# Phase 2 of a two-layer kernel: value products in three rounded passes, scalings and mixes moved to ScalarE, a new order on every engine

## The chip, the cores and the metric

The kernel runs on one core of one Trainium2 chip. The metric is device time in microseconds (us). The program is written as one instruction stream per engine: TensorE (PE in the profile; its weight loads are PEld), VectorE (DVE), ScalarE (ACT), GpSimd (POOL) and SyncE (SP), which only issues transfers here. Each stream runs strictly in its written order, and streams wait for each other through semaphores. TensorE writes only into PSUM, of which there are eight banks of 128 x 512 in float32.

## The reference

The input is 16 x 512 tokens of width 128. Everything that the change touches lies behind the slot softmax of the first layer, whose exponentials are ready when phase 2 begins. `_silu(y)` is y times sigmoid(y).

```python
xn = _layernorm(x)
Q = xn @ Wq + bq                      # K = V = Q, per sequence of 512 tokens
s = softmax(Q @ Q.T / sqrt(128)) @ Q
y = einsum('tznp,npH->tzH', C, Y_tilde)     # 2048 slots mixed into each token
x = x + s * _silu(y)
xn = _layernorm(x)
# layer 1, per sequence: gated linear recurrence
i_t, r_t = sigmoid(xn @ W_ig + b_ig), sigmoid(xn @ W_rg + b_rg)
a_t = exp(8 * r_t * log(sigmoid(lam) + 1e-8))
h_t = a_t * h_{t-1} + sqrt(1 - a_t**2 + 1e-6) * i_t * (xn @ W_in)
s = rmsnorm(h) @ W_out
xr = mu_r * xn + (1 - mu_r) * x_prev       # x_prev: xn one token earlier
xk = mu_k * xn + (1 - mu_k) * x_prev
g = sigmoid(xr @ W_r) * (relu(xk @ W_k)**2 @ W_v)
x = x + s * _silu(g)
```

## The kernel before

The work has three phases. The first two build the experts' outputs (`YHI`, `YLO`) and store the slot exponentials to device memory. Phase 2, which the change rewrites, starts at about 630 us of the profiled run and lasts to the end. It goes over 16 blocks of 512 tokens, software-pipelined: while TensorE mixes the slots of block n, the recurrence of blocks n-1 and n-2 is worked on.

For a block there are 16 chunks of 128 slots. Chunk c is loaded by SP, weighted by POOL (`exps_weighed`, two chunks at a time, line 142), turned by four transposes on TensorE into one of two PSUM banks `ct` (`exps_turned`, line 1094), rounded to float32r by ACT (`chunk_high`, line 1346, into a ring `chi` of RC = 4 buffers), its remainder taken by DVE (`chunk_low`, line 1505, into `clo`), and multiplied by three rounded matmuls (`combine`, lines 1104, 1105 and 1107: high x high, low x high, high x low). `exps_turned(c)` waits until `chunk_low(c - 2)` has released the bank.

Attention: `project` makes Q in bank `at[0]`, ACT copies it with the bias (`query`, line 1294), DVE rounds it (`project_split`), POOL takes the remainder (`query_low`), `values` (line 1126) turns it on TensorE into `at[1]` and waits for `query`; `scores(r)` are three rounded matmuls for each of four row groups, `row_max` (DVE), `probabilities` (ACT, Exp, line 1309, with a read of the row sum), `weights` (DVE reciprocal), `scaled` (DVE, line 1531), `turn(k)` transposes (line 1154), `turn_high(k)` (ACT copy, line 1317), `weigh(k)`: one float32 matmul (line 1164), which counts as two records.

Recurrence: `mean` (float32 matmul, line 1171), `centre` (DVE, line 1550), `squares`, `variance` (float32, line 1179), `deviation_log` (Ln, line 1356), `deviation_inverse` (Exp, line 1361), `normalise`, `normalised_split`, `normalised_low`, `difference` (POOL, line 1716), `mix_r`, `mix_k` (DVE, lines 1571 and 1578), three gate products of three rounded matmuls each (`decay_gate`, `input_gate`, `input_product`), float32 products `ffn_k`, `ffn_r`, `ffn_v`, `state_mean`, `state_out`, the scan (DVE, line 1614), and the pointwise steps on ACT (`decay_tanh`, `decay` (line 1373), `input_tanh` (line 1387), `input_log` (Ln, line 1417), `input_root` (Exp), `state_log` (Ln), `state_inverse`, `ffn_tanh`, ...).

The order of the streams is written out by hand or by a planner as five plain lists of calls in one loop per engine (lines 1070, 1230, 1451, 1645 and 1736); nothing reorders them.

## Time and profile before

| what | us |
|---|---|
| median of 3 runs | 1239.2 (1236.46 to 1244.97) |
| profiled execution, its own time | 1248.32 |
| its span, first to last instruction | 1246.5 |
| PE busy | 1162.2 (93%) |
| DVE busy | 1091.1 (88%) |
| ACT busy | 888.1 (71%) |
| POOL busy | 985.5 (79%) |

The busy time of an engine is a union of its instructions' durations. Instructions of one engine overlap by a little (the next starts before the one before has ended), so what an instruction costs its engine is read from start to start in the timeline, not from its duration. The granted TensorE clock averaged 0.972 of full speed over the span.

### The profile page before, as it was taken

Reading aid. Unit: us, or ns where it says so; the run is one execution under the profiler, and the core shown is the slowest. Engines: PE = TensorE matmul, PEld = TensorE weight load, DVE = VectorE, ACT = ScalarE, POOL = GpSimd, SP = SyncE. Lnnn points to the kernel's source line nnn. Section 1 sums busy time; section 2 is a strip of 40 time slices with the busy share of each in tenths; the row PEclk is TensorE's granted clock in tenths of the full one; section 3 lists DMA queues with packets and bytes.
Section 4 is the critical chain, followed back from the end, with each engine's and each line's share of the span. In section 5 each row is a group of like instructions: output and inputs, shape, how many; then the busy total and the mean of one; then the engine's idle time right before and its main releaser. Section 6 shows DMA issues by size and latency. Waiting matters only on the chain.

```text
span 1246.5 us, 17321 instructions
## 1 busy us (share of the span) xinstructions
PE 1162.2 (93%) x4994; PEld 776.7 (62%) x4994; DVE 1091.1 (88%) x1578; ACT 888.1 (71%) x2001; POOL 985.5 (79%) x790
## 2 busy tenths in 40 slices
PE   2799999999999999999689999999999999999984
PEld 2465556666666666665267777776677766777751
DVE  4799999999999999998457889999989889999873
ACT  4577777776766666666457887876787877788764
POOL 3499888999999999999467788877798777778720
PEclk9799999999999999999789999999999999999997
DMA  5444344443433434343734343434343434434310
GB/s 141 157 150 150 142 151 150 152 157 136 148 138 133 153 133 150 135 150 134 237 102 146 125 140 115 147 116 135 116 147 109 146 111 149 137 120 145 114 39 17
DMA packets 125486, 167.35 MB, mean 134 GB/s; under 512 B 7504, under 2 KB 101712, under 8 KB 125392
## 3 DMA queue, kind: packets, MB, share of 16 engines
q1 hardware_dynamic: 124720, 165.18, 39.7%
q10 hardware_dynamic: 672, 1.06, 0.3%
q8 instruction: 41, 0.67, 0.2%
q14 instruction: 53, 0.43, 0.1%
HBM read 90.71 MB, written 75.50 MB: 133 GB/s over the span
## 4 chain that ended last, share of the span: by engine, by line
PE 38%; DVE 7%; issue 4%; ACT 1%; POOL 0%; DVEq 0%; ACTq 0%; POOLq 0%
PE ct L1094 7%; PE at L1164 4%; PE yac L1107 4%; PE yac L1105 4%; PE yac L1104 4%; PE at L1154 2%; DVE b_e L1531 2%; DVE clo L1505 2%; PE lp L1210 1%; PE lp L1204 1%; PE lp L1216 1%; PE at L1143 1%; PE at L1142 1%; PE at L1140 1%; PE lp L1222 1%
## 5 line engine op out<-in xcount | busy, mean ns | idle before, releaser
L142 POOL TENSOR_TENSOR exp_slots_loaded<-exp_slots_loaded,slot_max 128x1024 f32<-128x1024 f32 x128 | 333.8, 2627 | 52.9 <-DMA exp_slots_loaded<-exp_slots 52.3
L813 POOL TENSOR_TENSOR dd<-ed,rz 128x512 f32<-128x512 f32 x256 | 264.7, 1050 | 39.5 <-ACT rz L659 37.7
L547 PE MATMUL acc<-dd,xns 128*128 128x512 f32 x512 | 262.5, 595 | 2.2 <-POOL dd L813 2.2
L1505 DVE TENSOR_TENSOR clo<-ct,chi 128x512 fp32r<-128x512 f32 x256 | 172.6, 679 | 58.6 <-ACT chi L1346 57.6
L824 POOL TENSOR_TENSOR ch<-exp_slots_loaded 128x512 f32<-128x512 f32 x128 | 164.1, 1282 | 26.7 <-ACT exp_slots_loaded L637 26.7
L751 DVE TENSOR_REDUCE mr<-lg 128x16 fp32r<-128x512 f32 x256 | 167.5, 686 | 19.9 <-PE lg L504 19.5
L628 ACT ACTIVATE ed<-lg 128x512 f32<-128x512 f32 x256 | 142.1, 594 | 55.7 <-PE lg L528 55.7
L637 ACT ACTIVATE exp_slots_loaded<-lg 128x512 f32<-128x512 f32 x256 | 147.9, 591 | 26.4 <-PE lg L535 23.3
L1346 ACT ACTIVATE chi<-ct 128x512 fp32r<-128x512 f32 x256 | 150.3, 594 | 20.3 <-PE ct L1094 19.2
L535 PE MATMUL lg<-shift_experts_to_slots,mt 128*128 128x512 f32 x256 | 162.7, 656 | 0.5 <-ACT ed L628 0.5
L1094 PEld LDWEIGHTS ct<-identity,exp_slots_loaded 128*128 128x128 f32 x1024 | 126.0, 142 | 57.7 <-issue 21.6
L1094 PE MATMUL ct<-identity,exp_slots_loaded 128*128 128x128 f32 x1024 | 153.0, 275 | 6.4 <-DVE clo L1505 3.5
L767 DVE TENSOR_REDUCE zd<-ed 128x32 f32<-128x1024 f32 x128 | 154.8, 1209 | 1.3 <-ACT ed L628 1.3
L760 DVE TENSOR_REDUCE mr<-lg 128x32 fp32r<-128x1024 f32 x128 | 155.8, 1217 | 0.0
L502 PE MATMUL lg<-phi_then_expert_out,xn_transposed 128*128 128x512 f32 x256 | 131.4, 513 | 12.3 <-PEq L395 12.0
L1104 PE MATMUL yac<-chi,phi_then_expert_out 128*128 128x512 f32 x256 | 132.6, 518 | 0.0
L547 PEld LDWEIGHTS acc<-dd,xns 128*128 128x128 f32 x512 | 94.1, 189 | 23.5 <-issue 3.9
L1107 PE MATMUL yac<-clo,phi_then_expert_out 128*128 128x512 f32 x256 | 102.5, 400 | 4.6 <-DVE clo L1505 4.6
L504 PE MATMUL lg<-phi_then_expert_out,xn_transposed 128*128 128x512 f32 x256 | 102.1, 399 | 0.0
L503 PE MATMUL lg<-phi_then_expert_out,xn_transposed 128*128 128x512 f32 x256 | 102.0, 398 | 0.0
L1105 PE MATMUL yac<-chi,phi_then_expert_out 128*128 128x512 f32 x256 | 101.9, 398 | 0.0
L535 PEld LDWEIGHTS lg<-shift_experts_to_slots,mt 128*128 128x128 f32 x256 | 48.3, 189 | 74.5 <-ACT ed L628 44.0
(200 smaller groups left out, 2435.5 us busy)
## 6 DMA issues: line engine op xcount, KB each, us to landing
exp_slots<-exp_slots_loaded SPq DMA_DIRECT2D x128, 512.0 KB, 2.8
exp_slots_loaded<-exp_slots SPq DMA_DIRECT2D x128, 512.0 KB, 3.9
xns<-xn_rows SPq DMA_DIRECT2D x128, 64.0 KB, 2.6
expert_w<-in_expert_w SPq DMA_DIRECT2D x8, 512.0 KB, 5.9
b_xraw<-in_xT SPq DMA_DIRECT2D x16, 256.0 KB, 3.7
out_t<-b_ti SPq DMA_DIRECT2D x16, 256.0 KB, 2.1
xn_rows<-slot_sum SPq DMA_DIRECT2D x8, 256.0 KB, 4.7
slot_sum<-in_x SPq DMA_DIRECT2D x2, 512.0 KB, 6.7
```

What stands on the lines that cost most here:

```text
L142: e.tensor_tensor(rows, rows, joined(SM, b)[:, h].unsqueeze(2).broadcast_to([P, TPB, GC * EPC, NP]), ALU.mult).then_inc(s_we)
L535: e.matmul(lg[v % 2][:, bank(k)], mt[v % 2][:, :], S2M[:, bank(k)], start=False, stop=True, skip_group_check=True).then_inc(s_s2)
L547: e.matmul(acc[k][:, :], xns[v % RX][:, :], dd[v % RX][:, bank(k)], start=tile == 0, stop=tile == NT - 1, skip_group_check=True).then_inc( ...
L751: e.tensor_reduce(mr[v % 2][:, k * HN // 2:(k + 1) * HN // 2], lg[v % 2][:, bank(k)].rearrange("q (n p) -> q n p", p=NP), AX_X, ALU.max).t ...
L760: e.tensor_reduce(mr[v % 2][:, HN:G], lg[v % 2][:, :].rearrange("q (n p) -> q p n", p=NP), AX_X, ALU.max).then_inc(s_mx)
L767: e.tensor_reduce(zd[v % 2][:, :], ed[v % RD][:, :].rearrange("q (n p) -> q n p", p=NP), AX_X, ALU.add).then_inc(s_zd)
L813: e.tensor_tensor(dd[v % RX][:, bank(k)].rearrange("q (n p) -> q n p", p=NP), ed[v % RD][:, bank(k)].rearrange("q (n p) -> q n p", p=NP), ...
L824: e.tensor_tensor(ch[v % 2][:, :], ec[v % RE][:, 0:BANK], ec[v % RE][:, BANK:HS], ALU.add).then_inc(s_ch)
L1094: done = e.transpose(ct[c % 2][:, rows(k)], ECL[:, g // GC % RL, k, c % GC * P:(c % GC + 1) * P], IDENT[:, :])
L1104: e.matmul(yac[:, :], YHI[:, c, :], chi[c % RC][:, :], start=c == 0, stop=False)
L1107: e.matmul(yac[:, :], YHI[:, c, :], clo[c % RC][:, :], start=False, stop=c == CH - 1).then_inc(c_y)
L1505: e.tensor_tensor(clo[c % RC][:, :], ct[c % 2][:, :], hi_f32(chi[c % RC][:, :]), ALU.subtract).then_inc(c_l)
```

## The change

It rewrites part of phase 2.

- `weigh(k)` becomes three rounded matmuls: the values and the turned probabilities are each kept as a rounded part and a remainder. New DVE steps take the remainders: `value_low` once and `turn_low` four times per block. `turn` and `values` now wait for the remainder (`kl`) where they waited for the copy (`kh`).
- `scaled` (four per block) moves from DVE to ACT.
- `mean` multiplies by identity minus mean, so its product is the centred input; `centre` is gone, and `squares` and `normalise` read PSUM.
- `difference` (POOL) is gone. ACT multiplies xn by mu (`scaled_r`, `scaled_k`), and DVE's `mix_r`, `mix_k` add (1 - mu) x_prev. Two small DVE instructions prepare 1 - mu before phase 2.
- `y_copy` is gone; `y_tanh` and `silu_y` read the accumulator `yac`, and the next block's `combine(0)` waits for `silu_y`.
- The rings `chi` and `clo` have 3 buffers in place of 4.
- All five orders are new; ACT's has two loads of the Ln set and two of the Tanh set per block in place of one each.

```diff
-            RC = 4
+            RC = 3
@@ combine
-                        e.wait_ge(y_c, i)
+                        e.wait_ge(S["u_y"], i)
@@ weigh
-                    e.matmul(at[0][:, :], B["vf"][:, rows(k)], pt[k % 2][:, :], start=k == 0, stop=k == TPB - 1).then_inc(A["w"])
+                    e.matmul(at[0][:, :], R["vh"][:, rows(k)], pth[k % 2][:, :], start=k == 0, stop=False)
+                    e.matmul(at[0][:, :], R["vl"][:, rows(k)], pth[k % 2][:, :], start=False, stop=False)
+                    e.wait_ge(A["kl"], i * TPB + k + 1)
+                    e.matmul(at[0][:, :], R["vh"][:, rows(k)], ptl[k % 2][:, :], start=False, stop=k == TPB - 1).then_inc(A["w"])
@@ mean
-                        e.matmul(lp[0][:, :], MEAN[:, :], B[f"x1{i % 2}"][:, :], start=True, stop=True).then_inc(S["mn"])
+                        e.matmul(lp[0][:, :], CENTRE, B[f"x1{i % 2}"][:, :], start=True, stop=True).then_inc(S["mn"])
@@ ScalarE: new
+                def scaled(i, r):
+                        e.wait_ge(A["z"], i * TPB + r + 1)
+                        e.activation(B[f"e{r}"][:, :], B[f"e{r}"][:, :], ACT.Identity, bias=one(EPS, 3),
+                                     scale=one(nmx, 4 * r + 3)).then_inc(A["p"])
+                def scaled_r(i):
+                        e.activation(B["xr"][:, :], x_in, ACT.Identity, bias=one(EPS, 3), scale=one(VEC, V_MUR)).then_inc(S["mr"])
...
@@ VectorE: new
+                def value_low(i):
+                        e.wait_ge(S["v_h"], i + 1)
+                        e.tensor_tensor(R["vl"][:, :], at[1][:, :], hi_f32(R["vh"][:, :]), ALU.subtract).then_inc(S["v_l"])
+                def turn_low(i, k):
+                        e.wait_ge(A["kh"], i * TPB + k + 1)
+                        e.tensor_tensor(ptl[k % 2][:, :], at[1][:, :], hi_f32(pth[k % 2][:, :]), ALU.subtract).then_inc(A["kl"])
...
```

The new order of TensorE, one round of its loop (n is the block whose slots are mixed; ET is `exps_turned`, C is `combine`):

```
C12(n-1) C13(n-1) turn2(n-1) ET15(n-1) decay_gate(n-2) C14(n-1) weigh1(n-1) turn3(n-1) C15(n-1)
weigh2(n-1) weigh3(n-1) ET0 input_gate(n-2) ET1 input_product(n-2) project C0 ET2 ffn_k(n-2)
values C1 ET3 C2 scores0 ET4 ET5 ffn_r(n-2) scores1 C3 scores2 ffn_v(n-2) ET6 C4 ET7 scores3
state_mean(n-2) ET8 C5 mean(n-1) C6 ET9 state_out(n-2) C7 variance(n-1) ET10 C8 turn0 ET11 C9
ET12 C10 turn1 ET13 weigh0 ET14 C11
```

The new order of ScalarE from the start of block n (CH is `chunk_high`):

```
CH0 CH1 input_tanh(n-2) log_table input_log(n-2) tanh_table query input_root(n-2) CH2 value_high CH3
CH4 ffn_k_relu(n-2) probabilities0 ffn_r_tanh(n-2) ffn_k_squares(n-2) CH5 next_factors
probabilities1 state_squares(n-2) CH6 scaled0 CH7 ffn_tanh(n-2) log_table probabilities2
state_log(n-2) scaled1 CH8 squares(n-1) probabilities3 state_inverse(n-2) CH9 scaled2 scaled3
deviation_log(n-1) tanh_table CH10 turn_high0 CH11 deviation_inverse(n-1) CH12 CH13 turn_high1 CH14
scaled_r(n-1) turn_high2 CH15 scaled_k(n-1) decay_tanh(n-1) decay(n-1) turn_high3 y_tanh
decay_squares(n-1) attended
```

## Rows read from the trace of the kernel before

**Rows 1.** Stretch of 15 blocks: us; PE, PEld, DVE, ACT, POOL busy; clock; DMA.

```profile
663.50:1206.30 542.80, 533.64 (x2649) 386.69 (x2648) 487.25 (x753) 425.32 (x770) 421.57 (x232) 1.00 0.40 128
```

**Rows 2.** Line 1331, one per block: durations ns min/median/max, first and last start us.

```profile
L1331 ACT ACTIVATE yt<-yac x16: 597/599/603, 663.5 to 1206.3; 128x512 f32<-128x512 f32 x16
```

**Rows 3.** Timeline of PE inside one block: start us, us, instruction, count.

```profile
825.93 0.60 PE L1094 MATMUL ct<-identity,exp_slots_loaded 128*128 128x128 f32 x4
826.37 1.02 PE L1164 MATMUL at<-pt,b_vf 128*128 128x512 f32 x2
827.23 0.60 PE L1094 MATMUL ct<-identity,exp_slots_loaded 128*128 128x128 f32 x4
...
828.76 0.39 PE L1111 MATMUL lp<-r_xl,weights_high 128*128 128x512 f32 x1
828.98 0.40 PE L1112 MATMUL lp<-r_xh,weights_low 128*128 128x512 f32 x1
829.22 0.40 PE L1104 MATMUL yac<-chi,phi_then_expert_out 128*128 128x512 f32 x1
```

**Rows 4.** Timeline of ACT around one table load.

```profile
841.51 0.62 ACT L1338 ACTIVATE b_ty<-yt 128x512 f32<-128x512 f32 x1
842.15 1.28 ACT L1445 ACT_TABLE_LOAD   x1
843.45 0.72 ACT L1417 ACTIVATE b_a<-b_a,epsilons 128x512 f32<-128x512 f32 x1
```

**Rows 5.** Lines of ACT over the same 15 blocks: count, busy us, mean ns, idle before.

```profile
L1445 ACT ACT_TABLE_LOAD x15 | 19.2, 1283 | 0.3
L1449 ACT ACT_TABLE_LOAD x15 | 19.2, 1283 | 0.3
L1373 ACT ACTIVATE b_aa<-b_aa,derived_vectors 128x512 f32<-128x512 f32 x15 | 12.2, 811 | 0.0
L1387 ACT ACTIVATE b_ti<-lp,derived_vectors 128x512 f32<-128x512 f32 x15 | 10.3, 690 | 14.3 <-PE lp L1112 14.3
```

**Rows 6.** Timelines of PE, ACT and DVE: what starts what.

```profile
866.14 0.60 PE L1094 MATMUL ct<-identity,exp_slots_loaded 128*128 128x128 f32 x4
...
866.77 0.60 ACT L1346 ACTIVATE chi<-ct 128x512 fp32r<-128x512 f32 x1 [0.65 <-PE ct L1094]
...
873.48 0.58 ACT L1346 ACTIVATE chi<-ct 128x512 fp32r<-128x512 f32 x1
...
874.09 0.69 DVE L1505 TENSOR_TENSOR clo<-ct,chi 128x512 fp32r<-128x512 f32 x1 [1.26 <-ACT chi L1346]
...
850.62 0.67 DVE L1505 TENSOR_TENSOR clo<-ct,chi 128x512 fp32r<-128x512 f32 x1
...
851.34 0.66 PE L1094 MATMUL ct<-identity,exp_slots_loaded 128*128 128x128 f32 x4 [1.46 <-DVE clo L1505]
```

**Rows 7.** Timeline of ACT, five instructions in a row without idle time.

```profile
853.49 0.69 ACT L1309 ACTIVATE b_e<-at,nmx 128x512 f32<-128x512 f32 x1
854.07 0.19 ACT L1309 ACTIVATION_READ_ACCUMULATOR b_e<-at,nmx 128x1 f32 x1
854.16 0.62 ACT L1351 ACTIVATE b_ty<-b_kr 128x512 f32<-128x512 f32 x1
854.69 0.68 ACT L1432 ACTIVATE b_aa<-lp,epsilons 128x512 f32<-128x512 f32 x1
855.26 1.08 ACT L1346 ACTIVATE chi<-ct 128x512 fp32r<-128x512 f32 x2
```

**Rows 8.** Three DVE lines that read SBUF: ns min/median/max.

```profile
L1531 DVE TENSOR_SCALAR b_e<-b_e,nmx x64: 469/485/2697, 641.8 to 1186.9; 128x512 f32<-128x512 f32 x64
L1578 DVE SCALAR_TENSOR_TENSOR b_xk<-weights,vectors,xn x16: 740/2882/2891, 684.7 to 1225.6; 128x512 f32<-128x512 f32 x16
L1614 DVE TENSOR_TENSOR_SCAN b_hh<-b_aa,vectors,b_ti x16: 1270/1272/3459, 702.9 to 1236.3; 128x512 f32<-128x512 f32 x16
```

**Rows 9.** Busy time by engine at the end of the run, columns as in the first group.

```profile
1200.00:1246.00 46.00, 23.85 (x57) 11.58 (x55) 18.45 (x27) 25.30 (x36) 3.51 (x3) 0.76 0.03 12
```

More of the change, by code:

```diff
@@ L1136, in scores @@
                     elif r == 1:
[L1137 removed]
+                        e.wait_ge(S["v_l"], i + 1)
                     else:
@@ L1286, in tensor2 @@
-                    combine(i + 1, 1)
+                    combine(i - 2, 12)
+                    combine(i - 2, 13)
+                    turn(i - 2, 2)
+                    exps_turned(i - 2, 15)
+                    decay_gate(i - 3)
+                    combine(i - 2, 14)
+                    weigh(i - 2, 1)
+                    turn(i - 2, 3)
+                    combine(i - 2, 15)
+                    weigh(i - 2, 2)
+                    weigh(i - 2, 3)
+                    exps_turned(i - 1, 0)
@@ new lines, in tensor2 @@
+                    input_gate(i - 3)
+                    exps_turned(i - 1, 1)
+                    input_product(i - 3)
+                    project(i - 1)
+                    combine(i - 1, 0)
+                    exps_turned(i - 1, 2)
+                    ffn_k(i - 3)
+                    values(i - 1)
+                    combine(i - 1, 1)
+                    exps_turned(i - 1, 3)
+                    combine(i - 1, 2)
+                    scores(i - 1, 0)
+                    exps_turned(i - 1, 4)
@@ new lines, in tensor2 @@
+                    mean(i - 2)
+                    combine(i - 1, 6)
+                    exps_turned(i - 1, 9)
+                    state_out(i - 3)
+                    combine(i - 1, 7)
+                    variance(i - 2)
+                    exps_turned(i - 1, 10)
+                    combine(i - 1, 8)
+                    turn(i - 1, 0)
+                    exps_turned(i - 1, 11)
+                    combine(i - 1, 9)
+                    exps_turned(i - 1, 12)
+                    combine(i - 1, 10)
@@ L1288, in scalar2 @@
+                    turn(i - 1, 1)
+                    exps_turned(i - 1, 13)
+                    weigh(i - 1, 0)
+                    exps_turned(i - 1, 14)
+                    combine(i - 1, 11)
             def scalar2(e):
@@ new lines, in scalar2 @@
+                    decay_tanh(i - 2)
+                    decay(i - 2)
+                    turn_high(i - 1, 3)
+                    y_tanh(i - 1)
+                    decay_squares(i - 2)
+                    attended(i - 1)
+                    chunk_high(i, 0)
+                    chunk_high(i, 1)
+                    input_tanh(i - 2)
+                    log_table(i - 1)
+                    input_log(i - 2)
+                    tanh_table(i - 1)
+                    query(i)
+                    input_root(i - 2)
@@ new lines, in scalar2 @@
+                    state_squares(i - 2)
+                    chunk_high(i, 6)
+                    scaled(i, 0)
+                    chunk_high(i, 7)
+                    ffn_tanh(i - 2)
+                    log_table(i - 1)
+                    probabilities(i, 2)
+                    state_log(i - 2)
+                    scaled(i, 1)
+                    chunk_high(i, 8)
+                    squares(i - 1)
+                    probabilities(i, 3)
+                    state_inverse(i - 2)
+                    chunk_high(i, 9)
@@ L1501, in vector2 @@
+                    scaled(i, 2)
+                    scaled(i, 3)
+                    deviation_log(i - 1)
+                    tanh_table(i - 1)
             def vector2(e):
```

327 lines of the change are left out of this document (125 added, 202 removed), and 4 rows, old and new, of the table S.

## The prediction

> **What bounds the kernel now.** First the block's length. The copy of the finished slot mix runs once per block, from 663.5 to 1206.3 us [rows 2], so 15 blocks take 542.8 us, 36.19 each. In that stretch PE is busy 533.6 of 542.8 us at full granted clock, DVE 487, ACT 425, POOL 422 [rows 1]. A busy PE need not be a packed PE, so I read the costs from start to start in PE's timeline [rows 3]: a group of four transposes takes 0.44 us (825.93 to 826.37), a float32 matmul of 512 columns 0.86 (826.37 to 827.23), a rounded one 0.23 (two in 829.22 - 828.76 = 0.46). A block has 21 groups of transposes, 72 rounded matmuls and 11 float32 ones: 21 x 0.44 + 72 x 0.23 + 11 x 0.86 = 9.24 + 16.56 + 9.46 = 35.26 us. So PE is packed but for 0.93 us per block. PE's own work is the bound, and the other engines matter only where they make it wait. The longest such wait that I found in the steady part is 1.46 us, for a `chunk_low` [rows 6], and the chain of waits alternates between PE and DVE.
>
> **The products.** Four `weigh` go from 0.86 to 3 x 0.23 = 0.69 us each. `mean` stays one float32 matmul. PE's sum becomes 21 x 0.44 + 84 x 0.23 + 7 x 0.86 = 34.58, a gain of 0.68 us per block. This is on the path.
>
> **VectorE** loses four `scaled`, mostly 0.485 us each but up to 2.70, and `centre` (about 0.68, as long as `chunk_low`); it gains five remainders at 0.68 [rows 6, 8]. That is 3.4 us added against 2.6 to 11.5 removed. It has 36.2 - 32.5 = 3.7 us free per block, so I take this as nothing: the cover is DVE's own idle time. POOL loses `difference`, also off the path, for POOL is idle 8 us per block [rows 1].
>
> **ScalarE** loses `y_copy` (0.48 from start to start, two copies in 1.08 us, the last of them 0.60 long [rows 7]). It gains four `scaled` and two mixes. No row shows ACT scaling from SBUF by a vector into SBUF with Identity; the nearest are Square, 0.53 from start to start [rows 7], and `decay` with a vector scale, 0.81 long [rows 5]. The plain copy's 0.48 is the floor. I take 0.53, the row that differs least, and keep 0.48 and 0.81. It also gains two table loads. A load is 1.28 us, there are two per block today [rows 5], and from its start to the next instruction's is 1.30; the Tanh ahead of it had taken 0.64 [rows 4]. In all ACT goes from 28.4 us busy per block to 28.4 - 0.48 + 6 x 0.53 + 2 x 1.30 = 33.7. That is under PE's 34.58 on average, but it is an ordered stream with many hand-offs to PE, so its place matters. I walk two stretches of it.
>
> **First stretch, `values`.** PE runs `values` only when `query` is through, and in ACT's new order `query` stands behind CH1, `input_tanh`, a load, `input_log` and a second load. On PE, from the start of ET1 to that of `values`, lie ET1, `input_product`, `project`, C0, ET2 and `ffn_k`: 2 x 0.44 + 9 x 0.23 + 0.86 = 3.81 us. On ACT: from the start of ET1 to CH1 0.63 (866.14 to 866.77), CH1 0.48, `input_tanh` 0.69 to its end, load 1.30, `input_log` 0.72, load 1.30, `query` 0.69, and 0.05 to wake PE (clo ends at 851.29, PE starts at 851.34): 5.86 us [rows 4 to 7]. PE waits 2.05 us in every block, and behind `values` C1 and ET3 wait with it. None of ACT's steps here can start earlier by another engine's doing, so this is the least it can be.
>
> **Second stretch, ET12.** ET12 needs `chunk_low(10)`, which needs CH10, which stands behind `deviation_log` and the second Tanh load. From ET4's start to ET12's PE has 9 groups of transposes, 30 rounded and 6 float32 matmuls: 3.96 + 6.90 + 5.16 = 16.02 us. ACT from ET4's start: 0.63, six chunk copies 2.88, four Exp of the probabilities 2.68 (0.67 each), four squares or Exp at 0.53 2.12, `ffn_k_relu` and `ffn_r_tanh` 0.96, `next_factors` 0.3 (half a copy's width, my estimate from 0.48), `ffn_tanh` 0.64, `state_log` 0.57, four `scaled` 2.12, `deviation_log` 0.69, two loads 2.60; then CH10 to its remainder 0.61 and on to PE 0.72 [rows 4 to 7]. Sum 17.52, so PE waits 1.50. With `scaled` at 0.48 it is 1.3, at 0.81 it is 2.6. The two stretches don't overlap on PE, so the waits add up.
>
> **Third stretch, `weigh(3)`.** From ET15 to the third pass of `weigh(3)` PE has 4.8 us (2 x 0.44 + 17 x 0.23). The way over ACT and DVE (0.63, CH15 0.48, `scaled_k` 0.53, `decay_tanh` 0.69, `decay` 0.81, copy and remainder 0.61 + 0.72) is 4.5, so it is covered by 0.3 us. But `mix_k` now stands ahead of `turn_low(3)` on DVE, and it takes 0.74 to 2.89 us, usually 2.88 [rows 8]; POOL weighs exponentials there in the new order as well. That can make PE up to 1.8 us late. I take 0.4 and keep 0 and 1.8.
>
> **Smaller edits.** The new waits on `kl` put one remainder (0.6 to 0.7 us) between `turn_high` and the next `turn`. With `turn0` to `turn1` 2.3 us of PE work apart and `turn1` to `turn2` 4 us, it is covered. With three buffers, CH(c) waits for C(c - 3); in the new order C(c - 3) stands ahead of ET(c) or at most one chunk behind it, so at worst CH14 is some 0.7 us late, 4 us before C14. `combine(0)` waits for `silu_y`, about 3 us after the tanh: covered. SP's order puts a load of x and a store among the exponentials' loads; the store waits for `output`, and the load behind it is weighed over 4 us later, so I count nothing. Today's 0.93 us of waits I take as swallowed by the new, longer ones, with 0.9 as the other end. Behind the last block the recurrence of two blocks runs alone, where ACT's steps are in series: two more loads 2.6, less `y_copy` 0.6: +2 once.
>
> **Sum.** A block takes 34.58 + 2.05 + 1.50 + 0.4 = 38.53 us against 36.19: +2.34, over 15 blocks +35, with the end +37. Against the profiled execution's own 1248.3 us this gives 1285; that execution is 9 us above the median of the runs, and against the median, 1239.2, it gives 1276.
>
> The Trainium skill (ScalarE: Activation LUTs, What ACT_TABLE_LOAD costs) speaks against the change more strongly: every switch of table set costs a load of about 1.28 us and a drain of about 1.38. Our load agrees (1.283), but the drain does not show, since the Tanh ahead of it had ended 0.02 us before the load began [rows 4].
>
> **Rivals.**
> - *PE still sets the pace, the other side.* ACT's loads fit between what PE waits for, or the second pair isn't in the program as the source has it. For it: ACT's mean demand, 33.7, is under 34.58. Against it: the first stretch would have to fall under 3.81 us, so that its two loads cost under 0.3 us each, and [rows 4] shows 1.30. Price: today's waits kept, -0.68 x 15 = -10, 1229; all waits gone, (36.19 - 34.58) x 15 = -24, 1215. Chance 0.16, two thirds of it at the faster end.
> - *Only `values` bites.* The second stretch is 9% over PE's work; if PE's matmuls between were slower than in [rows 3], by pieces that wait on DVE, it vanishes. 34.58 + 2.05 + 0.4 = 37.03, +13 + 2, 1254. Chance 0.12.
> - *DVE and POOL get in each other's way too.* `mix_k` makes PE wait 1.8, `scaled` costs 0.81, today's 0.93 stays: 34.58 + 2.05 + 2.6 + 1.8 + 0.9 = 41.9, +86, 1327 at the worst, 1301 halfway. For it: `scaled`, `mix_k` and the scan all have a second duration, 2.2 us longer [rows 8]. Against: `scaled` has left DVE. A wait above 2 us might also lower the granted clock, which is 1.00 over the blocks and 0.76 at the run's sparse end [rows 1, 9]. Chance 0.12.
> - *A drain at every load.* If the two new loads sit where ACT has more in flight, each load costs twice what it does here, 1.30 more: stretches of 8.5 and 20.1 us, waits of 4.7 and 4.1, 43.8 us per block, about 1355. It is the rule quoted above, and no row has it. Chance 0.02.
>
> **How the numbers follow.** The forecast has 0.58, its own range 1262 to 1300 from the ends kept above. The range 1245 to 1310 takes in the rival of the one wait and the nearer half of the DVE rival, and leaves out the faster ones and the far ends. About 1% can be told from no change, 1227 to 1252. Slower by over 1%: 0.58 + 0.12 + 0.02 + 0.07 of the one-wait rival = 0.79. Within: 0.05 of it and 0.05 of the first = 0.10. Faster: 0.11.
>
> **What would show it.** PE's idle time ahead of line `values` near 2 us per block, ended by ACT's `query`; idle time ahead of ET12 near 1.5 us, ended by `chunk_low`; four table loads per block, 1.30 us from start to start; the block at 38 to 39 us; PE's busy sum per block lower by about 0.7. I'd be wrong if `values` starts without idle time, if ACT shows gaps at its loads' places rather than PE, or if the block is under 36.2 us.

## The result: 7% slower, 53 us above the forecast

The changed kernel takes 1329.2 us (median of 4 runs, 1323.0 to 1333.4) against 1242.1 (4 runs, 1236.5 to 1245.0) of the kernel before: ratio 1.070, 95% interval 1.064 to 1.077. The forecast was 1276, the range 1245 to 1310, so the sign was right, and the size, +37 us, was less than half of the +87 measured. The profiled execution took 1323.0 us, span 1321.2. Two executions below, one of the kernel before and one of `one_pair`, fell into a slower state of about 2400 us and are left out.

First the block's length, by the tanh that reads y from PSUM (it took the place of the copy in [rows 2]), then the busy time between its first and last occurrence (columns: stretch; us; PE, PEld, DVE, ACT, POOL busy; clock; DMA share; GB/s):

```profile
L1344 ACT ACTIVATE b_ty<-yac x16: 597/599/601, 653.5 to 1278.0; 128x512 f32<-128x512 f32 x16
```

```profile
653.50:1278.00 624.50, 552.25 (x2715) 402.25 (x2715) 491.40 (x754) 510.61 (x873) 398.02 (x219) 0.98 0.35 111
```

Fifteen blocks take 624.5 us, 41.63 each, against 36.19 [rows 1, 2]; all but three are 41.5 to 41.8. The first of these tanhs comes 10 us earlier than the first copy did, and what follows the last one is 3 us longer: -10 + 81.7 + 3 = 74.7 us, with 81.7 = 624.5 - 542.8, which is the difference of the two spans (1321.2 - 1246.5). PE is busy 552 of 624.5 us, where it was busy 534 of 543. So it idles 4.8 us per block, where it idled 0.6.

What PE waits for in the changed kernel from 660 to 1280 us (what waits, what it waits for: us in total, times, longest):

```profile
PE at L1128 <- ACT b_qf L1301: 28.8, 15, 2.1
PE ct L1096 <- DVE clo L1532: 25.6, 14, 1.8
PE yac L1109 <- DVE clo L1532: 6.4, 9, 0.7
PE at L1156 <- ACT b_e L1336: 5.2, 14, 0.4
PE lp L1186 <- ACT b_ty L1357: 2.2, 9, 0.3
```

The same view of the kernel before, over its 15 blocks:

```profile
PE yac L1107 <- DVE clo L1505: 4.3, 11, 0.4
PE ct L1094 <- DVE clo L1505: 2.8, 2, 1.5
PE at L1154 <- DVE b_e L1531: 1.5, 7, 0.3
```

The first two lines of the changed kernel are the forecast's two stretches, `values` behind `query` and ET12 behind `chunk_low(10)`. The others were not in the sum.

**The first stretch** on ACT's timeline, and the two instructions of PE on either side of the wait:

```profile
905.71 0.68 ACT L1407 ACTIVATE b_ti<-lp,derived_vectors 128x512 f32<-128x512 f32 x1
906.41 1.28 ACT L1465 ACT_TABLE_LOAD   x1
907.70 0.72 ACT L1437 ACTIVATE b_a<-b_a,epsilons 128x512 f32<-128x512 f32 x1
908.44 1.28 ACT L1469 ACT_TABLE_LOAD   x1
909.74 0.69 ACT L1301 ACTIVATE b_qf<-at,vectors 128x512 f32<-128x512 f32 x1
```

```profile
907.54 1.02 PE L1211 MATMUL lp<-b_xk,weights 128*128 128x512 f32 x2
910.48 0.65 PE L1128 MATMUL at<-identity,b_qf 128*128 128x128 f32 x4 [1.92 <-ACT b_qf L1301]
```

The two matmuls that start at 907.54 cost 0.86, so `values` could start at 908.40 and starts at 910.48: 2.08 us late, forecast 2.05. Each load delays the next instruction by 1.29 or 1.30 us, as in [rows 4]. The second load is followed by `query` without anything more, so the drain of about 1.38 us that the Trainium skill (ScalarE: Activation LUTs, What ACT_TABLE_LOAD costs) puts beside each switch does not show here either.

**The second stretch** goes from 914.49 (ET4) to 934.13 (ET12):

```profile
914.49 1.04 PE L1096 MATMUL ct<-identity,exp_slots_loaded 128*128 128x128 f32 x8
...
934.13 0.63 PE L1096 MATMUL ct<-identity,exp_slots_loaded 128*128 128x128 f32 x4 [1.83 <-DVE clo L1532]
```

```profile
919.86 0.69 ACT L1316 ACTIVATE b_e<-at,nmx 128x512 f32<-128x512 f32 x1 [1.19 <-DVE nmx L1548]
...
921.54 0.81 ACT L1336 ACTIVATE b_e<-b_e,epsilons,nmx 128x512 f32<-128x512 f32 x1
922.25 0.59 ACT L1352 ACTIVATE chi<-ct 128x512 fp32r<-128x512 f32 x1
...
931.37 1.28 ACT L1469 ACT_TABLE_LOAD   x1
932.66 0.60 ACT L1352 ACTIVATE chi<-ct 128x512 fp32r<-128x512 f32 x1
```

That is 19.64 us where the forecast had 17.52 for ACT's way. PE's own work between the two is 16.09 us, by the same two groups in the kernel without any loads (`no_loads`, below; forecast 16.02):

```profile
866.71 1.03 PE L1096 MATMUL ct<-identity,exp_slots_loaded 128*128 128x128 f32 x8
...
882.80 0.60 PE L1096 MATMUL ct<-identity,exp_slots_loaded 128*128 128x128 f32 x4
```

So PE comes 3.55 us late over this stretch, not 1.50. Start by start against `no_loads`, 2.1 of it arise at ET12, 0.6 at the first turn, 0.5 at `variance` and 0.4 in small pieces. Two differences on ACT's way can be read off. ACT stands idle for 1.19 us ahead of the second probability, which waits for its row maximum. And `scaled` costs 0.71 from start to start (921.54 to 922.25) and is 0.81 long; the forecast had 0.53. That is 0.7 us over the four of a block.

Why the row maximum is late shows on DVE and POOL:

```profile
910.98 1.82 DVE L1627 SCALAR_TENSOR_TENSOR b_ti<-b_ti,b_a 128x512 f32<-128x512 f32 x1
912.73 0.68 DVE L1532 TENSOR_TENSOR clo<-ct,chi 128x512 fp32r<-128x512 f32 x1
...
915.52 2.94 DVE L1635 TENSOR_TENSOR_SCAN b_hh<-b_aa,vectors,b_ti 128x512 f32<-128x512 f32 x1
...
918.96 0.68 DVE L1544 TENSOR_REDUCE nmx<-at 128x1 f32<-128x512 f32 x1
```

```profile
910.96 1.29 POOL L1720 TENSOR_TENSOR r_ql<-b_qf,r_qh 128x512 fp32r<-128x512 f32 x1 [3.86 <-DVE r_qh L1539]
912.21 5.17 POOL L142 TENSOR_TENSOR exp_slots_loaded<-exp_slots_loaded,slot_max 128x1024 f32<-128x1024 f32 x2
```

`scan_input` starts 0.02 us behind POOL's `query_low`, which lasts until 912.25, and takes 1.82 us. The `chunk_low(2)` behind it makes PE wait 0.7 us (the third line of the waits). The scan falls into POOL's weighing and takes 2.94 us, where its short form is 1.27 [rows 8]; `row_max(1)` is behind it.

Why `scan_input` comes just behind `query_low`: it needs `input_root`, which stands directly behind the late `query` on ACT and ends at 910.94.

```profile
910.32 0.62 ACT L1442 ACTIVATE b_a<-b_a 128x512 f32<-128x512 f32 x1
```

### The profile page after: what moved, and what is told of

The parts are those of the page before. It is cut to its first block, busy times and chain, and to the rows that moved or that the text cites. A ratio compares the mean times of both kernels' runs of the same rounds, so it can differ in the third digit from the quotient of the medians.

```text
span 1321.2 us, 17509 instructions
## 1 busy us (share of the span) xinstructions
PE 1176.8 (89%) x5058; PEld 789.9 (60%) x5058; DVE 1094.0 (83%) x1581; ACT 983.8 (74%) x2117; POOL 959.1 (73%) x774
## 3 DMA queue, kind: packets, MB, share of 16 engines
q10 hardware_dynamic: 672, 1.06, 0.3%
## 4 chain that ended last, share of the span: by engine, by line
ACT 18%; PE 14%; DVE 10%; issue 9%; POOL 1%; ACTq 0%; POOLq 0%
PE ct L1096 4%; ACT L1465 3%; ACT chi L1352 3%; DVE clo L1532 3%; PE yac L1109 2%; ACT L1469 2%; ACT b_e L1336 2%; ACT b_e L1316 1%; PE yac L1106 1%; PE yac L1107 1%; DVE ptl L1563 1%; DVE b_ti L1627 1%; PE at L1156 1%; DVE b_xk L1599 1%; DVE b_xr L1594 1%
## 5 line engine op out<-in xcount | busy, mean ns | idle before, releaser
L142 POOL TENSOR_TENSOR exp_slots_loaded<-exp_slots_loaded,slot_max 128x1024 f32<-128x1024 f32 x128 | 326.1, 2567 | 14.7 <-DMA exp_slots_loaded<-exp_slots 14.3
L813 POOL TENSOR_TENSOR dd<-ed,rz 128x512 f32<-128x512 f32 x256 | 264.6, 1050 | 39.5 <-ACT rz L659 37.7
L1352 ACT ACTIVATE chi<-ct 128x512 fp32r<-128x512 f32 x256 | 153.0, 598 | 89.0 <-PE ct L1096 75.0
L1096 PE MATMUL ct<-identity,exp_slots_loaded 128*128 128x128 f32 x1024 | 157.2, 280 | 30.3 <-DVE clo L1532 25.6
```

The source lines that it names most:

```text
L142: e.tensor_tensor(rows, rows, joined(SM, b)[:, h].unsqueeze(2).broadcast_to([P, TPB, GC * EPC, NP]), ALU.mult).then_inc(s_we)
L813: e.tensor_tensor(dd[v % RX][:, bank(k)].rearrange("q (n p) -> q n p", p=NP), ed[v % RD][:, bank(k)].rearrange("q (n p) -> q n p", p=NP), ...
L1096: done = e.transpose(ct[c % 2][:, rows(k)], ECL[:, g // GC % RL, k, c % GC * P:(c % GC + 1) * P], IDENT[:, :])
L1352: e.activation(chi[c % RC][:, :], ct[c % 2][:, :], ACT.Copy).then_inc(c_h)
```

## The experiments

Each is an edit of the changed kernel unless it says otherwise. "Block" is the steady distance between two y tanhs; the changed kernel's is 41.8, the one before's 36.5.

### Take the loads away

`no_first_loads`, `no_second_loads` and `no_loads` (both edits together, one Tanh load ahead of the loop). They leave out the logarithms, so they do not compute the reference.

```
# no_first_loads
-  log_table(i - 1)
   input_log(i - 2)          # Ln becomes Identity
-  tanh_table(i - 1)
# no_second_loads
-  log_table(i - 1)
   state_log(i - 2)          # Ln becomes Identity
   ...
   deviation_log(i - 1)      # Ln becomes Identity
-  tanh_table(i - 1)
```

> The changed kernel without the first pair of table loads (the Ln load ahead of input_log and the Tanh load behind it). So that no set is missing, input_log computes Identity with the same bias in place of Ln, so the output is not the reference's; all else is as in the changed kernel. Theory A (ScalarE's loads set PE's waits, each where it stands): query starts 2.6 us earlier, PE's wait ahead of values (2.06 us per block) goes to nothing, the block falls from 41.6 to about 39.5 us, the run by about 30 us, near 1298. The waits of the second stretch, ET4 to ET12, stay at 3.6 us. Theory B (VectorE and GpSimd hold each other up, and the loads only fill time that ACT would wait anyway): the wait ahead of values goes, but PE waits as much longer at the next hand-off, and the run stays within 10 us of the changed kernel's.

> The changed kernel without the second pair of loads (Ln ahead of probabilities2, Tanh behind deviation_log); state_log and deviation_log compute Identity in place of Ln, so the output is not the reference's. Theory A: ACT reaches chunk_high(10) 2.6 us earlier, of the 3.6 us that PE waits between ET4 and ET12 some 1.0 us stays, the block falls to about 39.0 us, the run by 35 to 40 us, near 1291; the wait ahead of values stays at 2.06. Theory B: PE's waits move to turn0 (behind scaled) or to other remainders, within 10 us of the changed kernel's time.

> The changed kernel with neither pair (one Tanh load ahead of the loop); all three Ln are Identity, so the output is not the reference's. Theory A: the two gains add up, since the stretches do not overlap on PE: 41.6 - 2.06 - 2.6 = about 37.0 us per block, a run of about 1258, 70 us below the changed kernel and still above the kernel before, because scaled on ACT, the scan behind GpSimd's weighing and chunk_low(2) behind scan_input keep 2 us of waits. Theory B: less than 25 us below the changed kernel.

| kernel | median us | ratio to before, 95% | block us |
|---|---|---|---|
| no_first_loads | 1248.2 | 1.004 (1.001 to 1.006) | 37.4 |
| no_second_loads | 1274.0 | 1.026 (1.023 to 1.029) | 39.1 |
| no_loads | 1205.4 | 0.971 (0.968 to 0.973) | 35.05 |

The main wait of PE in `no_first_loads`, then in `no_second_loads`:

```profile
PE ct L1096 <- DVE clo L1530: 23.8, 13, 1.8
```

```profile
PE at L1128 <- ACT b_qf L1301: 27.0, 14, 2.1
```

Each pair owns its own wait, as the forecast had it, and they all but add up (4.4 and 2.7 us per block, 6.75 together). But the first pair is worth more than twice its wait of 2.1. All three ran faster than expected: `no_first_loads` was expected at 39.5 us per block and 1298 us, `no_second_loads` at 39.0 and 1291, `no_loads` at 37.0 and 1258. Without both pairs PE is all but packed at 35.05, and everything else of the change is a gain of 3%.

Where the first pair's other 2.3 us come from shows in `no_first_loads`, on DVE and POOL and in PE's second stretch:

```profile
878.88 0.68 DVE L1625 SCALAR_TENSOR_TENSOR b_ti<-b_ti,b_a 128x512 f32<-128x512 f32 x1
...
882.72 1.42 DVE L1633 TENSOR_TENSOR_SCAN b_hh<-b_aa,vectors,b_ti 128x512 f32<-128x512 f32 x1
```

```profile
879.04 1.67 POOL L1718 TENSOR_TENSOR r_ql<-b_qf,r_qh 128x512 fp32r<-128x512 f32 x1 [1.07 <-DVE r_qh L1537]
```

```profile
881.68 1.04 PE L1096 MATMUL ct<-identity,exp_slots_loaded 128*128 128x128 f32 x8
...
900.08 0.63 PE L1096 MATMUL ct<-identity,exp_slots_loaded 128*128 128x128 f32 x4 [1.84 <-DVE clo L1530]
```

`input_root` is ready early here, so `scan_input` follows at once and starts 0.16 us ahead of `query_low`. The two still meet, but now it is POOL that waits: `scan_input` takes 0.68 us and `query_low` 1.67 instead of 1.29. The scan takes 1.42. C2's wait for `chunk_low(2)` is gone (0.9 us per block), and ET4 to ET12 takes 18.40 us instead of 19.64. These 0.9 and 1.24 us are the first pair's excess, but for 0.2: it is what the pair triggers between DVE and POOL.

### The products by themselves

`no_loads_one_pass` is `no_loads` with the values' products in one float32 pass again:

```
-  e.matmul(at[0][:, :], R["vh"][:, rows(k)], pth[k % 2][:, :], ...)
-  e.matmul(at[0][:, :], R["vl"][:, rows(k)], pth[k % 2][:, :], ...)
-  e.matmul(at[0][:, :], R["vh"][:, rows(k)], ptl[k % 2][:, :], ...)
+  e.matmul(at[0][:, :], B["vf"][:, rows(k)], pt[k % 2][:, :], ...)
```

> The kernel without loads (three Ln as Identity, so the output is not the reference's) with the products undone: weigh is one float32 matmul again, value_low and turn_low are left out. In the run without loads PE is packed, so the three rounded passes are worth their start-to-start difference there: 4 x (0.86 - 0.69) = 0.68 us per block, and this kernel should be 10 us slower than no_loads, near 1215. If the remainders or their waits cost PE something, it would be less than 6 us slower, or faster.

1213.1 us against 1205.4 of `no_loads`: the three passes gain 7.7 us, a steady 0.38 per block (35.43 against 35.05) rather than 0.68. The gain is real and small. What is missing stands at `weigh(3)` in `no_loads`, where the weight load of the third pass waits for `turn_low(3)`:

```profile
858.05 0.40 PE L1167 MATMUL at<-pth,r_vl 128*128 128x512 f32 x1
...
858.44 0.19 PEld L1169 LDWEIGHTS at<-ptl,r_vh 128*128 128x128 f32 x1 [0.43 <-DVE ptl L1560]
858.45 0.50 PE L1169 MATMUL at<-ptl,r_vh 128*128 128x512 f32 x1
```

The second pass costs 0.40 and the third 0.34 (the next instruction starts at 858.79), where each costs 0.23 elsewhere: 0.28 us per block. With three passes at 0.70 (869.13 to 869.83 in the same kernel), that gives 4 x (0.86 - 0.70) - 0.28 = 0.36.

An attempt with the products in the order and with the loads of the kernel before was:

```
-  e.matmul(at[0][:, :], B["vf"][:, rows(k)], pt[k % 2][:, :], ...)
+  # three rounded passes, as above; on DVE value_low and turn_low, three buffers for chi and clo
```

> The kernel before with one part of the change: weigh in three rounded matmuls, with value_low and turn_low on VectorE, in the order of before (RC = 3 for room; the second remainder buffer shares the room of the query's remainder). Theory A: PE's own work falls by 0.68 us per block, but turn(1) and turn(2) stand only 1.1 and 1.4 us of PE work behind the turn before them and now wait for copy and remainder, 2.0 us, so PE waits 0.9 + 0.6 us more: a block of 36.2 - 0.7 + 0.9 to 1.5, a run 3 to 12 us above the kernel before. If VectorE's five added remainders (3.0 us on an engine that is busy 32.5 of 36.2) were the changed kernel's trouble, this kernel would be 25 us or more above the kernel before.

It ran 1411.3 us, 169 above the kernel before, where Theory A had 3 to 12. From 660 to 1200 us PE waits 63 us for `chunk_low` in 57 places (longest 3.4). By the letter of its expectation this speaks for VectorE's five added remainders as the trouble. But it also has three buffers, remainders at new places in the old order and a remainder that shares the query's room, and it does not compute the reference's output; and `no_loads` has all five remainders and a block of 35.05. What in this mixture costs the 169 us was not taken apart.

### Move single waits

`query_ahead` puts `query` ahead of the first load. `dve_order` puts `scan_input` two remainders later and the scan behind `row_max(1)`. `one_pair` gathers both Ln parts behind one pair of loads, for which it also exchanges `ffn_k` and `ffn_r` on TensorE and moves `ffn_k_relu`, `state_squares`, `ffn_tanh`, `ffn_silu` and `gate_second`; `one_pair_dve_order` joins the two.

```
# query_ahead                      # dve_order
+  query(i)                        -  scan_input(i - 2)
   log_table(i - 1)                   chunk_low(i, 2)
   input_log(i - 2)                   value_low(i)
   tanh_table(i - 1)               +  scan_input(i - 2)
-  query(i)                        ...
                                   -  scan(i - 2)
                                      chunk_low(i, 4)
                                      row_max(i, 1)
                                   +  scan(i - 2)
# one_pair, on ACT, in part
-  log_table(i - 1)
-  input_log(i - 2)
-  tanh_table(i - 1)
   query(i)
-  input_root(i - 2)
   chunk_high(i, 2)
+  ffn_r_tanh(i - 2)
+  log_table(i - 1)
   chunk_high(i, 3)
   value_high(i)
+  input_log(i - 2)
+  input_root(i - 2)
...
-  log_table(i - 1)                # ahead of state_log
```

> The changed kernel with one call moved in ScalarE's order: query ahead of the first pair of loads in place of behind it. Both pairs stay. Theory A (what counts is what stands behind a load): values no longer waits, but CH2 stands where it stood, and the way from ET1 over ScalarE to C2 is 6.9 us against 5.4 us of PE work, so some 1.5 us of the 2.06 come back ahead of C2. Theory C (the second cost of the first loads is a collision: query sets off GpSimd's query_low at the moment in which scan_input starts on VectorE, 1.82 us in place of 0.68, and the scan then meets the weighing, 2.77 in place of 1.43): that collision goes too, since query_low then runs 3 us before scan_input. With C the block falls from 41.6 to 39.5 us or less (run near 1293); without C only to 41 (run near 1318).

> The changed kernel with two calls moved in VectorE's order: scan_input behind chunk_low(2) and value_low, and the scan behind row_max(1) in place of ahead of it. All loads stay. Theory C: C2 no longer waits for chunk_low(2) (0.9 us per block), and probabilities1 no longer waits 1.2 us for row_max(1) behind a scan of 2.8 us, so the block falls by up to 2 us, to about 39.6, and the run by up to 30 us, to near 1298. If the collisions with GpSimd are without effect on PE, the run stays within 8 us of the changed kernel.

> The changed kernel with a new order that needs one pair of loads per block, all of the computation kept: query, CH2 and ffn_r_tanh ahead of the Ln load, ffn_r and ffn_k exchanged on TensorE, all three Ln in one stretch, one Tanh load behind deviation_log, and ffn_tanh, ffn_silu and gate_second after it. Theory A: the run without loads has a block of 34.65 us, PE's own work; one pair costs only where a hand-off has under 1.3 us to spare. I expect 34.7 to 36 us per block, a run of 1206 to 1226, below the kernel before. Theory B would leave the block above 36.2.

> The one-pair order with VectorE's two calls moved as in dve_order. If the scan and scan_input still collide with GpSimd in the one-pair order, this is 5 to 15 us faster than one_pair; if PE is packed there already, the two are the same within 4 us.

| kernel | median us | ratio, 95% | what PE waits for |
|---|---|---|---|
| query_ahead | 1337.5 | 1.073 (1.067 to 1.080) | `values` gone; C2 for `chunk_high(2)` up to 1.7, ET12 up to 1.8 |
| dve_order | 1320.6 | 1.063 (1.060 to 1.067) | `values` 2.1; ET5 and ET12 for `chunk_low`, 32.1 us in 18 |
| one_pair | 1399.1 | 1.126 (1.123 to 1.129) | C2 for `chunk_low(2)` up to 5.2 |
| one_pair_dve_order | 1368.4 | 1.101 (1.099 to 1.104) | `chunk_low` up to 3.9, remainder of the probabilities 24.9 in 11 |

Expected were 1293 or 1318 us for `query_ahead`, near 1298 for `dve_order` and 1206 to 1226 for `one_pair`. None is more than 0.7% below the changed kernel, and `one_pair` is 70 us above it. `one_pair_dve_order` was expected 5 to 15 us below `one_pair`, or within 4, and is 31 below. One wait taken away comes back at the next hand-off. Nor did any of the four take the collision away: `scan_input` still starts while POOL weighs, and lasts 1.56 us in the median in `query_ahead`, 2.28 in `one_pair`, 2.32 in `one_pair_dve_order` and, longer than the changed kernel's 1.82, 2.47 in `dve_order`.

```profile
L1627 DVE SCALAR_TENSOR_TENSOR b_ti<-b_ti,b_a x16: 692/2466/2484, 700.2 to 1302.6; 128x512 f32<-128x512 f32 x16
```

In `dve_order` it now stands ahead of `chunk_low(3)`, for which ET5 waits 1.7 us. So these four misses do not say that DVE's order is without effect.

### The loads where ACT is idle, and scaled on VectorE

`loads_in_gaps` has `query` ahead of the first load, the first Tanh load behind `chunk_high(3)`, and `deviation_log` with the second Tanh load in the next block, between the chunks 10 and 13. `scaled_on_vector` gives the four `scaled` back to DVE in the changed kernel; `gaps_and_scaled_vector` does both.

```
# scaled_on_vector, on DVE in place of ACT
+  e.tensor_scalar(B[f"e{r}"][:, :], B[f"e{r}"][:, :], one(nmx, 4 * r + 3), None, ALU.mult)
# loads_in_gaps, in part
+  query(i)
   log_table(i - 1)
   input_log(i - 2)
-  tanh_table(i - 1)
-  query(i)
   input_root(i - 2)
   chunk_high(i, 2)
   value_high(i)
   chunk_high(i, 3)
+  tanh_table(i - 1)
```

> The changed kernel with all four loads kept but moved in ScalarE's order to places where it waits for PE in the run without loads: query ahead of the first Ln load, the first Tanh load behind CH3 (1.2 us idle ahead of CH4), deviation_log behind turn_high(0), the second Tanh load behind CH12 (1.0 us idle ahead of CH13). Theory A (a load costs what its place leaves uncovered): values and ET12 wait little, C2 some 0.6 us; a block of 36.5 to 38 us against 41.8, a run of 1237 to 1260. If a load cost the same wherever it stands, the block would stay near 41.8 and the run near 1325.

> The changed kernel with one part undone: scaled on VectorE again (a tensor_scalar behind the next chunk_low), all loads kept. ScalarE loses four instructions of 0.71 us from start to start in the stretch from ET4 to ET12. Theory A: PE's waits ahead of turn(0) and ET12 (0.6 and 2.0 us per block) shrink by up to 2.6 us, the block falls from 41.8 to 39.5 or 40, the run to near 1295. Rival: VectorE, which scaled left, meets GpSimd's weighing up to 2.2 us at a time and takes back more than half of it, a run above 1312.

> The order of loads_in_gaps with scaled on VectorE. Theory A: with ScalarE relieved of 2.8 us in the second stretch PE's waits there go, a block of 35.5 to 36.5 us and a run of 1215 to 1235, below the kernel before by up to 2%. If GpSimd's collisions decide, it is no faster than loads_in_gaps.

They ran 1294.7 (ratio 1.043, 1.037 to 1.048), 1291.2 (1.040, 1.035 to 1.044) and 1292.3 us (1.041, 1.037 to 1.045). So either edit alone, the loads' place or `scaled`, is worth 35 to 38 us, and the two together are worth no more than one. Expected were 1237 to 1260, near 1295, and 1215 to 1235 us; the last came out as its expectation has it if the collisions decide, and `scan_input` lasts 2.85 us in it. In `scaled_on_vector` the steady block is 39.95: ACT's four `scaled` cost 1.85 us per block. In `loads_in_gaps` it is 40.95, only 0.85 less than the changed kernel's; the rest of its gain lies in the first block, in two blocks of 44.2 us that it does not have, and at both ends. With the loads in the gaps one wait stands out, that of C2's third pass for `chunk_low(2)`, and the granted clock of a steady block is 0.96 (columns as above, PE alone):

```profile
PE yac L1109 <- DVE clo L1532: 29.5, 13, 2.3
```

```profile
741.00:782.00 41.00, 37.62 (x183) 0.96 0.36 116
```

The lower clock follows this wait: 3.4 us of each block are at the lower level, in which PE's instructions fall another 1.7 us behind those of `no_loads`.

### The scan input out of the remainders' way

Three steps on VectorE, on top of `loads_in_gaps`: `low_ahead_of_scan_input`, then `scan_behind_row_max`, then `scan_input_behind_row_max`.

```
# low_ahead_of_scan_input          # scan_input_behind_row_max (all three steps)
   project_split(i)                   project_split(i)
-  scan_input(i - 2)                  chunk_low(i, 2)
   chunk_low(i, 2)                    value_low(i)
   value_low(i)                       chunk_low(i, 3)
   chunk_low(i, 3)                    row_max(i, 0)
+  scan_input(i - 2)                  chunk_low(i, 4)
   row_max(i, 0)                      row_max(i, 1)
   scan(i - 2)                        scan_input(i - 2)
   chunk_low(i, 4)                    scan(i - 2)
   row_max(i, 1)                      weights(i, 0)
```

> The kernel loads_in_gaps (both pairs of table loads moved to where ScalarE is idle; steady block 40.95 us, 1294.7 us) with the scan input moved on VectorE from ahead of chunk_low(2), value_low and chunk_low(3) to behind them. In loads_in_gaps the only large wait of PE is the third pass of the second projection for chunk_low(2), up to 2.3 us, 29.5 us in 13 blocks, and it begins as the scan input runs beside POOL. Theory (the collision on VectorE, and the half-clock stretch that follows its wait, are the rest of the miss): that wait goes, the PEclk in the steady part returns above 0.98, and the block falls by 2.3 us of wait and 1 to 2 us of clock to 36.7 to 37.7 us; run 1230 to 1250 us. Rival (a wait that moves): the scan comes 2 us later, the row maxima behind it are late, and PE waits for the weights instead: block 40 to 41, run 1280 to 1300. Rival (the loads themselves cost it): no change either, without a new wait on VectorE.

> The kernel low_ahead_of_scan_input with the scan, too, moved on VectorE behind chunk_low(4) and row_max(1). Theory (collision): prob0 and prob1 no longer wait for nmx behind a scan of 2.7 us; the gain over low_ahead_of_scan_input is what PE waits there for nmx and clo, 0 to 1.2 us a block: 0 to 20 us of the run, 1215 to 1250 us. Rival (a wait that moves): ffn and the row maxima 2 and 3 come 2.7 us later in their turn, and PE waits at a later probability or at the state's product: 1250 to 1300 us.

> The kernel scan_behind_row_max with the scan input moved on VectorE behind row_max(0), chunk_low(4) and row_max(1), directly ahead of the scan. In scan_behind_row_max the blocks are 39.2 us where the scan input beside POOL lasts 2.92 us, and 37.1 us where it lasts 0.68 to 0.89, and PE waits 1.4 us at the third scores in the first kind alone. Theory (what was left of the miss was this collision): nothing that PE needs is behind the scan input now, all blocks are near 37.1 us with both pairs of table loads in, 9 or 10 blocks gain 2.1 us each: 1263 to 1250 less about 19, a run of 1240 to 1255 us, within 1% of before. Rival (a wait that moves): the scan comes later or collides with POOL's next weighing, and chunk_low(5) behind it is late by 1 to 2 us: blocks 38.5 to 40, run 1260 to 1280 us.

| kernel | median us | ratio to before, 95% | block us | longest steady wait |
|---|---|---|---|---|
| loads_in_gaps | 1294.7 | 1.043 (1.037 to 1.048) | 40.95 | C2, 2.3 |
| low_ahead_of_scan_input | 1275.3 | 1.026 (1.024 to 1.029) | 39.32 | scores, 1.4 |
| scan_behind_row_max | 1268.4 | 1.022 (1.019 to 1.025) | 39.2 or 37.1 | scores, 1.4 |
| scan_input_behind_row_max | 1259.1 | 1.015 (1.010 to 1.020) | 37.75 | under 1 |

The main wait of `low_ahead_of_scan_input`, and one steady block's clock:

```profile
PE at L1142 <- ACT b_e L1316: 19.6, 14, 1.4
```

```profile
741.00:782.00 41.00, 38.23 (x192) 1.00 0.40 126
```

The clock came back as expected, the block fell by 1.6 us rather than 3.3 to 4.3, and a wait moved to the third scores, behind `row_max(0)`, which is now behind the long `scan_input`: the rival of a wait that moves held for half of it. `scan_behind_row_max` gained 7 us more, of 0 to 20 expected, and stays above the 1215 to 1250 us of its theory. It gives the cleanest evidence of all, since one program shows both kinds of block. Two blocks, start to end (columns as in [rows 1]):

```profile
876.30:915.40 39.10, 36.40 (x183) 26.43 (x182) 32.58 (x52) 34.33 (x59) 26.99 (x15) 1.00 0.38 121
954.60:991.70 37.10, 36.00 (x183) 26.62 (x183) 30.69 (x52) 34.38 (x60) 27.41 (x17) 1.00 0.42 131
```

The instruction in each of them:

```profile
886.65 2.92 DVE L1627 SCALAR_TENSOR_TENSOR b_ti<-b_ti,b_a 128x512 f32<-128x512 f32 x1
...
965.04 0.73 DVE L1627 SCALAR_TENSOR_TENSOR b_ti<-b_ti,b_a 128x512 f32<-128x512 f32 x1
```

And POOL's two weighings nearest to each (durations ns min/median/max, first and last start):

```profile
L142 POOL TENSOR_TENSOR exp_slots_loaded<-exp_slots_loaded,slot_max x2: 2378/2388/2397, 884.3 to 886.6; 128x1024 f32<-128x1024 f32 x2
...
L142 POOL TENSOR_TENSOR exp_slots_loaded<-exp_slots_loaded,slot_max x2: 2392/2620/2848, 962.8 to 965.2; 128x1024 f32<-128x1024 f32 x2
```

In the first block POOL's second weighing starts at the moment at which `scan_input` does, lasts until 889.03, and `scan_input` ends at 889.57: 2.38 + 0.54. In the second block `scan_input` starts 0.1 us ahead of the weighing, takes its own time, and the weighing takes 2.85 instead of 2.38. The two do not share, one waits for the other. Among the 14 blocks behind the first, the eight with a `scan_input` of 2.91 to 2.94 us last 39.2, and the five with 0.68 to 0.89 last 37.0 to 37.1; the last one has 2.93 and 40.6. Of the 2.1 us between the kinds PE loses 1.55 at the third scores (idle 1.4).

That is a rule of the Trainium skill (SBUF — State Buffer, SBUF: two separate sides): a VectorE operation with two SBUF inputs and a GpSimd operation that reads SBUF take one pair of ports as a lock for the whole instruction, and the one that starts first blocks the other. The durations here agree (2.92 against 0.73, 2.85 against 2.38). Which of the two is first can be read only where the starts are apart, as by the 0.1 us here or the 0.16 in `no_first_loads`: with starts within 0.02 us the records don't tell. POOL's record is ahead by 0.01 us at 886.65, where `scan_input` waits, and by 0.02 at 1002.11 in the same kernel, where it takes its 0.68 and the weighing 2.96.

In the last kernel all blocks but the first and the last are 37.6 to 37.8, its `scan_input` is short but for one near the end, and its waits are small but for long ones at the end:

```profile
L1627 DVE SCALAR_TENSOR_TENSOR b_ti<-b_ti,b_a x16: 691/692/1854, 697.7 to 1243.0; 128x512 f32<-128x512 f32 x16
```

```profile
PE ct L1096 <- DVE clo L1532: 12.4, 27, 3.3
PE yac L1106 <- ACT chi L1352: 5.7, 14, 0.4
PE at L1156 <- ACT b_e L1336: 4.4, 13, 0.4
```

It is 70 us faster than the changed kernel with the same instructions, and 1.5% slower than the one before. Expected were blocks of 37.1 and 1240 to 1255 us. The blocks have 37.75, 2.7 more than in `no_loads`: C2 comes 0.7 us late (for `chunk_high(2)`), ET7, behind the scan, 0.3, the first turn 0.5 and ET12 0.8, the rest in small pieces. No version with all of the computation in place beat the kernel before.

## Why the forecast had the sign and not the size

- **PE's sum.** Forecast 34.58 us per block; `no_loads` has 35.05. Of the 0.47 between, 0.28 stands at `weigh(3)` (the third stretch) and the rest in the rounding of the prices: three rounded passes cost 0.70, not 0.69, which is some 0.28 over 84 passes, and a group of transposes 0.435, not 0.44, which takes 0.1 back.
- **The products**, forecast -0.68: measured -0.38 (steady) in `no_loads_one_pass` against `no_loads`. On the path, as said, less the 0.28 of `weigh(3)`.
- **First stretch**, forecast 2.05: 2.08 on the timeline, 2.1 in the waits. Right.
- **Second stretch**, forecast 1.50: 3.55 late from ET4 to ET12. Ahead of it C2 is 0.9 late, for which the sum had nothing. **This is the step that failed**, together with the sentence ahead of it that took VectorE's part as nothing because DVE has 3.7 us free per block. The walk went over ACT alone. Two hand-offs come back from DVE, `row_max(1)` and `chunk_low(2)`, and in the new order both are behind an instruction of the recurrence that reads SBUF while POOL does. Without the first pair of loads, where these instructions are short, the stretch is 1.24 us shorter and C2's 0.9 are gone; `scaled` is another 0.7. [rows 8] had such durations, 2.88 against 0.74 for `mix_k` and 3.46 against 1.27 for the scan. They were read for `mix_k` in the third stretch and not for the scan and `scan_input`, which stand at two worse places. `scan_input` itself is 0.68 us in the median and 1.06 at most in the kernel before, so its own row would not have warned; what warns is that it has two SBUF inputs, as `mix_k` has.
- **`scaled`** at 0.53 from start to start: 0.71. The row that I put as an end, `decay` with a vector scale at 0.81, was the right neighbour: Identity with a vector as its scale, SBUF to SBUF, is 0.82 long. It takes 16 x 4 x 0.71 = 45 us of ACT's time, and `scaled_on_vector` won 38 of them back, 28 in the steady blocks (15 x 1.85).
- **Third stretch**, forecast 0.4: 0.3 late in eleven of the 15 blocks, 0.28 in `no_loads`. Right, and by the wait that was named, `turn_low(3)` behind `mix_k`.
- **The end**, forecast +2 once: +3.0.
- **The start**, not in the sum: 10 us earlier. It was not taken apart.

Sum in a steady block: 35.05 of `no_loads` + 6.75 of waits and late starts, 41.8. Forecast were 34.58 + 3.95. Of the 3.3 us between, the second stretch has 2.05, C2 0.9, the prices 0.2 and small pieces the rest. The mean over all 15 blocks, 41.63, is 3.1 above the forecast.

The rival that came true is the third, DVE and POOL in each other's way too, with a chance of 0.12. That its block, 41.9, and its time at the worst, 1327, are what was measured is luck: it adds 1.8 us for `mix_k`, where 0.3 was measured, and today's 0.9 us of waits, and it has neither C2's 0.9 nor the 1.24 of the second stretch. Its mechanism was right and its place wrong: `scan_input` and the scan make PE wait, `mix_k` hardly. That `scaled` left DVE, my argument against the rival, says nothing about the instructions that stay. Its remark on the clock bears out in the records. PE's clock behind a wait of 1.83 us, of the changed kernel:

```profile
890.00:893.40 3.40, 3.17 (x12) 0.50 0.16 56
```

That is the lower of the two levels, 1.2 GHz, for this stretch, and a matmul that costs 0.23 costs 0.43 there. It decides little in the changed kernel: the same waits left the clock at 1.00 in seven of the 15 blocks, and blocks at 1.00 and at 0.96 are both 41.8 long. Where the slow stretch follows the wait of `values`, C2's wait is gone from the block; in two blocks it follows ET12's wait, and these are 44.2 long, 5 us in all.

The drain rival, 1355, fell by the first stretch alone, and so did the rival in which PE keeps the lead. Only without any loads does it keep it, at 1205.

**What stays open.** How much of the 6.75 us belongs to the loads and how much to the collision has no single answer. Taking the loads away gives 6.75 and takes the collision with it. Moving the loads and then the recurrence's two instructions gives 4.05, moving the loads alone 0.85. The final order of VectorE with the loads in their old places was not run: `dve_order`, which gives 0.3, still has a `scan_input` of 2.47 us. The last kernel with `scaled` on VectorE was not run either. Why either `scaled` on VectorE or the loads in the gaps gains 35 to 38 us and both no more was not traced further than to the C2 wait of 2.3 us that is left in the second and the third of those kernels.

## What to carry to other kernels

When a step moves off an engine, that engine's share of free time is no cover: walk the whole way from one PE instruction to the next over every engine that hands something back, with the longest duration that each instruction, or one with operands like it, shows, and not with the median alone. Where VectorE and GpSimd both read SBUF, place VectorE's two-input SBUF operations behind the remainders and row maxima that PE needs, never ahead of them: the same instruction cost 0.7 or 2.9 us by a start of 0.1 us sooner or later. And a table load cost its 1.28 to 1.30 us here and no more, but its place in an ordered stream costs also what becomes late and meets something else.

## What the runs showed of the hardware

- A VectorE operation with two SBUF inputs that starts while POOL weighs ends 0.54 us after POOL's instruction does (886.65 to 889.57, POOL's end 889.03). The scan at 915.52 ends 1.1 us after POOL's (912.21 + 5.17 = 917.38). Where VectorE starts first, POOL's instruction is the longer one, by 0.46 us (2.85 against 2.39) or 0.38 (`query_low`, 1.67 against 1.29). VectorE operations that read PSUM stay at 0.68 us through all of this.
- ACT's Identity with a per-partition vector as scale, SBUF to SBUF, 128x512: 0.82 us long and 0.71 from start to start, against 0.60 and 0.48 for a plain copy from PSUM.
- Directly behind four transposes a rounded matmul shows 0.32 us from start to start rather than 0.23 (871.74 to 872.06 in `no_loads`), but the group ahead of it shows 0.35 rather than 0.44 (871.39 to 871.74). The two together cost 0.67 us either way: prices read from start to start hold for the sum, not for each record.
